# A graph layer with its iterations written out, six groups of places for gathered rows, and the last block of nodes finished early

## The reference

```python
h = jnp.maximum(_layernorm(x, axis=-1), 0.0)
out = h @ W_root + bias
for r in range(8):
    m = (edge_type == r).astype(h.dtype)
    msg = h[src] @ W[r] * m[:, None]
    agg = jax.ops.segment_sum(msg, dst, num_segments=6250)
    cnt = jax.ops.segment_sum(m, dst, num_segments=6250)
    out = out + agg / jnp.maximum(cnt, 1.0)[:, None]
return x + out
```

## Time and profile before

| | |
|---|---|
| time, median of 3 runs | 1579.58 us (1576.46 to 1584.89) |
| the profiled execution, its own time | 1583.01 us |
| its span | 1581.3 us |
| TensorE matmul busy | 753.3 us, 48% |
| weight load busy | 637.7 us, 40% |
| VectorE busy | 729.5 us, 46% |
| ScalarE busy | 511.6 us, 32% |
| GpSimd busy | 758.0 us, 48% |
| mean granted TensorE clock | 0.684 of full |
| row transfers of the late tiles (L464) | 1523 |
| indirect gathers of main tiles | 789 |

### The profile page before, as it was taken

How to read it: one execution, slowest core, us unless ns; L and a number is a source line. 1 busy time by engine, 2 the same in 40 slices (tenths; PEclk the granted TensorE clock), 3 DMA queues, 4 the chain that set the end, 5 groups by cost and what they waited for, 6 DMA issues and landing times.

```text
span 1581.3 us, 24568 instructions
## 1 busy us (share of the span) xinstructions
PE 753.3 (48%) x4265; PEld 637.7 (40%) x4265; DVE 729.5 (46%) x2320; ACT 511.6 (32%) x1183; POOL 758.0 (48%) x809
## 2 busy tenths in 40 slices
PE   0347575574774375466420555645501746742016
PEld 0236454454564254355320444544400545632016
DVE  4747576565564345454420354544510545442007
ACT  3744443433343133343310133433300334331001
POOL 6464566565565365565530255566510566563000
PEclk9967777776676676776755667677655767575556
DMA  6461111111111011111110011111100111111000
GB/s 201 135 151 30 46 43 47 43 48 44 43 44 44 26 44 40 43 45 43 42 29 6 20 44 45 39 43 45 41 19 6 38 44 43 44 44 27 5 7 12
DMA packets 54308, 71.31 MB, mean 45 GB/s; under 512 B 15214, under 2 KB 39550, under 8 KB 54222
## 3 DMA queue, kind: packets, MB, share of 16 engines
q0 software_dynamic: 25248, 51.76, 12.4%
q1 hardware_dynamic: 28974, 18.69, 4.2%
HBM read 63.99 MB, written 6.40 MB: 45 GB/s over the span
## 4 chain that ended last, share of the span: by engine, by line
SPq 54%; issue 36%; DVE 4%; another core or an unknown queue 3%; PE 2%; ACT 1%; DMA 0%; DVEq 0%; POOL 0%; POOLq 0%
SPq L464 46%; SPq L458 6%; PE acc L1620 1%; SPq L450 1%; PE fin L1653 1%; DVE onehot L1106 1%; SPq L443 1%; DVE ring L1120 1%; ACT h_all L625 0%; DMA x_all<-in_x 0%; DVE t_stats L856 0%; DVE stats L835 0%; DVE x_all L1248 0%; PE acc L1624 0%
## 5 line engine op out<-in xcount | busy, mean ns | idle before, releaser
L556 POOL DMA_INDIRECT hg<-h_table,idx x729 | 696.4, 955 | 742.3 <-ACT idx L669 545.7
L1620 PE MATMUL acc<-onehot,hg 128*128 128x104 f32 (+2 forms) x1578 | 454.3, 408 | 104.0 <-issue 43.2
L1620 PEld LDWEIGHTS acc<-onehot,hg 128*128 128x128 f32 x1578 | 325.7, 256 | 153.6 <-issue 74.3
L669 ACT ACTIVATE idx<-src_i 128x3 int32 (+1 forms) x243 | 48.1, 198 | 818.2 <-PE acc L1627 427.6
L1200 DVE SCALAR_TENSOR_TENSOR fin<-ring,zp 128x472 f32<-128x472 f32 x100 | 65.2, 652 | 452.3 <-PE zp L1635 285.7
L1106 DVE TENSOR_SCALAR onehot<-iota,key_f 128x104 f32<-128x104 f32 (+2 forms) x789 | 231.1, 314 | 54.8 <-issue 31.2
L1624 PE MATMUL acc<-onehot,ones_bf 128*128 128x104 bf16 (+2 forms) x789 | 220.6, 280 | 12.0 <-issue 12.0
L1120 DVE TENSOR_TENSOR ring<-ring,acc 128x512 f32 x263 | 178.4, 678 | 96.2 <-remote 40.0
L1642 PE MATMUL zp<-ident,cnt_row 1*118 1x1 f32 x400 | 44.3, 227 | 335.3 <-issue 182.3
L1248 DVE SCALAR_TENSOR_TENSOR x_all<-fin,inv,x_all 118x128 f32 (+1 forms) x400 | 136.8, 342 | 108.0 <-remote 100.4
L1642 PEld LDWEIGHTS zp<-ident,cnt_row 1*118 1x118 f32 x400 | 41.4, 197 | 348.3 <-issue 348.3
(11 more groups left out here) (165 smaller groups left out, 485.9 us busy)
## 6 DMA issues: line engine op xcount, KB each, us to landing
hg<-h_table SPq DMA_DIRECT2D x1523, 0.5 KB
hg<-h_table,idx POOLq DMA_INDIRECT x729
out<-x_all SPq DMA_DIRECT2D x52, 59.0 KB
x_all<-in_x SPq DMA_DIRECT2D x7, 384.0 KB, 3.7
h_table<-h_all SPq DMA_DIRECT2D x7, 384.0 KB
h_all<-h_table SPq DMA_DIRECT2D x5, 504.0 KB
x_all<-in_x SPq DMA_DIRECT2D x5, 504.0 KB
late_src<-in_src SPq DMA_DIRECT2D x47, 0.1 KB
```

Source lines behind the costliest of these rows:

```text
L556: nc.gpsimd.indirect_dma_start(out=hg[:, j, :], out_offset=None, in_=table, in_offset=bass.IndirectOffsetOnAxis(ap=idx[:, j:j + 1], axis=0 ...
L1620: nc.tensor.matmul(both[:, 0, :, a:e], hg[:, slot, :], hot.rearrange("p (r n) -> p r n", r=R), start=(j == 0), stop=(j == n - 1), skip_gro ...
```

## The change

- All iterations are written out: no loops, waits on constants; the `settled` increments are gone from them.
- `hg` holds ten groups first (`FIRST`), then six (`DEEP`) in places 0 to 17; the late tiles use places 18 to 29. POOL waits for `group_summed` itself and reads its indices from `src_i`; `stage` and `idx` are gone. SP begins the late fetch at 10 groups.
- SP fetches two pieces instead of one ahead of every eighth store (`FETCH_MORE`).
- `BLK` is 119, so the last block (number 52) has 62 nodes instead of 114. `LATE_AT` becomes 20, 31, 42, 47. The last block is made from `late_ring` alone in iterations 48 to 50; its neighbours' part of `late_ring` is joined in iteration 51. The block before the last three is finished in `iteration` and no longer in `end`.
- The copies of own rows (`own`) and of counts (`take_counts`) are gone: TensorE reads `h_all` and `ring`.
- ScalarE makes `zeros` and clears the first columns of `ring`; before, POOL and VectorE did.
- The flag that the inputs fit this kernel's plan is made in iteration 16 instead of in the last.

```diff
-BLK = 118
+BLK = 119
-LATE_AT = (20, 31, 42, 51)
+LATE_AT = (20, 31, 42, ENDI - 5)
+LAST_MADE, LAST_LOW, LAST_HIGH, LATE_JOINED = range(ENDI - 4, ENDI)
+FETCH_MORE = 8
+FIRST = 2 * GROUPS
+DEEP = 2 * GROUPS - LATE_GROUPS
...
+        def user_before(g):
+            return g - FIRST if g < FIRST + DEEP else g - DEEP
+        def slot_of(t):
+            return t if t < FIRST * GT else (t - FIRST * GT) % (DEEP * GT)
...
-            for first, last in zip((STATICS,) + tuple(at + 1 for at in LATE_AT[:-1]), LATE_AT):
-                with eng.Fori(first, last) as i:
-                    iteration(i)
-                iteration(last)
+            for i in range(STATICS, ENDI):
+                iteration(i)
             end()
...
-            sp.wait_ge(group_summed, (AHEAD - 1) * GROUPS)
-            for b in range(BLOCKS):
-                if b < chunks_of_late:
-                    fetch_rows(b)
-                store(b, BLK if b < BLOCKS - 1 else LASTN)
+            sp.wait_ge(group_summed, FIRST)
+            fetched = 0
+            for b in range(LASTB):
+                for _ in range(2 if b % FETCH_MORE == FETCH_MORE - 1 else 1):
+                    if fetched < chunks_of_late:
+                        fetch_rows(fetched)
+                        fetched += 1
+                if b == ENDB:
+                    sp.wait_ge(late_step, TERM_STEPS + R + 1)
+                    sp.dma_start(out[LASTB * BLK:N, :], x_all[0:LASTN, LASTB, :]).then_inc(stored, 16)
+                store(b, BLK)
...
+            for t in range(MAIN):
+                g = t // GT
+                if t % GT == 0:
+                    if g == XG:
+                        pool.wait_ge(h_stored, H_STORES)
...
+                    if user_before(g) >= 0:
+                        pool.wait_ge(group_summed, user_before(g) + 1)
+                nc.gpsimd.indirect_dma_start(
+                    out=hg[:, slot_of(t), :], out_offset=None, in_=x if g < XG else table,
+                    in_offset=bass.IndirectOffsetOnAxis(ap=src_i[:, t:t + 1], axis=0)).then_inc(gathered[slot_of(t)], 16)
...
+            nc.scalar.activation(zeros[:, :], eps[:, :].to_broadcast([P, SEG]), ACT.Copy, scale=0.0).then_inc(table_loaded, 1)
+            clear_columns(0)
-            def stage(g, q, ahead):
-                act.wait_ge(group_summed, g + 1)
...
-                nc.scalar.activation(idx[:, q * GT:(q + 1) * GT], src_i[:, bass.ds((g + ahead) * GT, GT)],
-                                     ACT.Copy).then_inc(idx_ready, 1)
...
-            nc.vector.memset(ring[:, :, :, ZERO_CUTS[0]:ZERO_CUTS[1]], 0.0).then_inc(ring_cleared, 1)
...
+                    if static(i, LAST_MADE) and q == 1:
+                        make_late_block(i)
+                    if static(i, LAST_MADE) and q == 3:
+                        late_inverses()
+                    if static(i, LAST_LOW) and q == 3:
+                        add_late_terms(0)
+                    if static(i, LAST_HIGH) and q == 3:
+                        add_late_terms(1)
+                    if static(i, LATE_JOINED) and q == 0:
+                        join_late()
...
+                    if static(i, LAST_MADE) and q == 2:
+                        late_counts()
+                    if static(i, LAST_MADE) and q == 3:
+                        pe.wait_ge(late_step, BLOCK_STEPS + 2)
+                    if static(i, LAST_LOW) and q == 2:
+                        late_relations(0, i)
+                    if static(i, LAST_LOW) and q == 3:
+                        pe.wait_ge(late_step, TERM_STEPS + R // 2)
+                    if static(i, LAST_HIGH) and q == 2:
+                        late_relations(1, i)
+                    if static(i, LAST_HIGH) and q == 3:
+                        pe.wait_ge(late_step, TERM_STEPS + R)
+            def late_relations(half, i):
+                pe.wait_ge(late_step, BLOCK_STEPS)
+                pe.wait_ge(group_added, i * GROUPS - 1)
+                for r in range(half * (R // 2), (half + 1) * (R // 2)):
+                    at = (r % (R // 2)) * F
+                    last = nc.tensor.matmul(last_z[:, at:at + F], last_blk[:, r, :], w_sb[:, r, :], start=True, stop=True)
+                last.then_inc(late_mm, 1)
```

More of the change, by code:

```diff
@@ L549, in gathers @@
[L549 to L557, removed]
-                        in_offset=bass.IndirectOffsetOnAxis(ap=idx[:, j:j + 1], axis=0)).then_inc(gathered[j], 16)
-            pool.wait_ge(src0_i, 1)
@@ L596, in _, with clear_columns @@
             act.wait_ge(table_loaded, 1)
+            nc.scalar.activation(zeros[:, :], eps[:, :].to_broadcast([P, SEG]), ACT.Copy, scale=0.0).then_inc(table_loaded, 1)
+            act.wait_ge(table_loaded, 2)
+            def clear_columns(step):
+                at = slice(ZERO_CUTS[step], ZERO_CUTS[step + 1])
+                for a in range(2):
+                    nc.scalar.activation(ring[:, a, :, at], zeros[:, 0:at.stop - at.start].unsqueeze(1)
+                                         .to_broadcast([P, R, at.stop - at.start]), ACT.Copy).then_inc(ring_cleared, 1)
+            clear_columns(0)
             def deviations(k):
@@ L626, in _ @@
                                          scale=rstd[:, c:c + 1]).then_inc(h_ready, 1)
-            def clear_columns(step):
-                at = slice(ZERO_CUTS[step], ZERO_CUTS[step + 1])
-                for a in range(2):
-                    nc.scalar.activation(ring[:, a, :, at], zeros[:, 0:at.stop - at.start].unsqueeze(1)
-                                         .to_broadcast([P, R, at.stop - at.start]), ACT.Copy).then_inc(ring_cleared, 1)
-            act.wait_ge(fills_made, 1)
             clear_columns(1)
@@ L740, in iteration @@
                 b = block_of(i, LAG)
-                slot = slot_of(b) if b is not None else None
+                slot = ring_slot(b) if b is not None else None
                 for q in range(GROUPS):
@@ L1414, in make_last_block @@
                     dve.wait_ge(blk_made, 2 * b + half)
-                    nc.vector.scalar_tensor_tensor(out=tail_own, in0=ring[:, 1, rs, slot], scalar=LOOP_FLAG / 2, in1=h_b,
+                    nc.vector.scalar_tensor_tensor(out=own, in0=ring[:, 1, rs, slot], scalar=LOOP_FLAG / 2, in1=h_b,
                                                    op0=ALU.is_ge, op1=ALU.mult).then_inc(own_part_made, 1)
-                    dve.wait_ge(z_done, b)
+                    if k != 1:
+                        dve.wait_ge(z_done, b if k == 0 else b - 1)
@@ L1706, in iteration @@
                         tail_products()
+                    if static(i, STATICS - 1) and q == 3:
+                        pe.wait_ge(bad_ready, 1)
+                        pe.wait_ge(group_added, i * GROUPS)
+                        nc.tensor.matmul(badT, bad1[:, :], ones[:, 0:1], start=True, stop=True).then_inc(tail_mm, 1)
                     if part_at(i, q, 3, 1) is not None:
@@ new lines, in last_relations @@
+            def last_relations(k, half):
+                b = TAILB[k]
+                pe.wait_ge(blk_made, 2 * b + 2 if k == 0 else 2 * b + half + 1)
+                if half:
+                    pe.wait_ge(y_ready, b)
+                else:
+                    pe.wait_ge(term_added, terms_before(b - 1) + (R // 2 + 1 if k == 0 else R // 2))
+                for r in range(half * (R // 2), (half + 1) * (R // 2)):
+                    at = (r % (R // 2)) * F
+                    last = nc.tensor.matmul(fin[0:BLK, half, at:at + F], tail_blk[k][:, r, :], w_sb[:, r, :],
+                                            start=True, stop=True)
+                last.then_inc(z_high if half else z_low, 1)
@@ new lines, in late_counts @@
+            def late_counts():
+                pe.wait_ge(late_step, BLOCK_STEPS)
+                for r in range(R):
+                    last = nc.tensor.transpose(last_cntT[:, r:r + 1], late_ring[0:1, 1, r, LAST_AT:LATE_NODES], ident[0:1, 0:1])
+                last.then_inc(late_mm, 1)
+            def late_relations(half, i):
+                pe.wait_ge(late_step, BLOCK_STEPS)
+                pe.wait_ge(group_added, i * GROUPS - 1)
+                for r in range(half * (R // 2), (half + 1) * (R // 2)):
+                    at = (r % (R // 2)) * F
+                    last = nc.tensor.matmul(last_z[:, at:at + F], last_blk[:, r, :], w_sb[:, r, :], start=True, stop=True)
+                last.then_inc(late_mm, 1)
```

345 lines of the change are left out of this document (170 added, 175 removed).

## The result

The changed kernel took 1521.08 us as a median of four executions (1501.4 to 1540.7), the kernel before 1578.02 us on the same chip (1576.36 to 1584.89). The medians' ratio is 0.964; the ratio of 0.955, with an interval of 0.946 to 0.964, leaves out the two executions (1527.3 and 1540.7) that lie over 1.5% above the fastest. The forecast was 1583 us with a range of 1552 to 1622. The profiled execution of the changed kernel is the longest of its four, 1540.7 us with a span of 1538.9, so all that is read from its trace is read from a slow one of them.

A forecast was written before the change was run, and what follows sets the result against it. SP's fetch of the late rows, slowed by gathers, was taken to bound the kernel. Terms -29.8 - 33.6 - 7.4 + 76 - 2 = +3.2 gave a 1584.5 us span, 1583 us on the median's footing; range 1552 to 1622.

The forecast's parts named there:

- The bound: SP's fetch of the last 1523 edges' rows sets the time from 138.5 to 1531.5 us.
- The beginning of the fetch: SP's late fetch waits for 10 groups summed instead of 20 and begins near 108 us: -29.8 us.
- The overlap: Gathers colliding with SP's fetch fall from 711 to 672, with 60 behind it: -33.6 us.
- The price of a gather: SP's delay per colliding gather, 0.861 us before, taken as 0.85 after: -7.4 us; bounds 0.81 and 0.91.
- The footing: The sum starts from the profiled execution, 3.4 us above its median; 1586 us becomes 1583 us on the median's footing.
- The tail: The stretch behind SP's fetch grows from 49.8 to 125.5 us, with 26 groups standing there: +76 us.
- the other engines' traffic makes SP slow: Loops' register instructions and `settled` increments slow SP; removal might halve a gather's price, -286 us, about 1330 us; chance 0.06.
- my two counter-arguments: Against traffic slowing SP: SP stays at 0.70 us while TensorE stands still; the first 17 iterations without loops cost 0.81.
- a cheaper gather: A gather costs SP 0.81 us (-27), or the tail nears 95 us (-30): 1550 to 1565 us; chance 0.25.
- The signs of being wrong: Pieces under gathers below 33 us on average, the 26 groups under 100 us, or SP waiting for stores.
- The speed of the iterations: Faster hand-overs save 1.2 us an iteration, five times behind SP's fetch, -6 us; in the other 47 TensorE only waits longer.
- The rule of the Trainium skill cited in the prediction: Taken branches outside the two-page window cost a fetch; by it all 36 looped iterations gain, -36 us instead of -6.

The follow-up runs named there:

- e18: The changed kernel with the 12 late tiles gathered by GpSimd and SP's 1523 row transfers left out: 1229.12 us, 0.778 of the kernel before.
- e13: The kernel before with its loops written out and without the `settled` increments: 1512.14 us, 0.958 of the kernel before.
- e10: The kernel before with each of SP's 1523 row transfers issued a second time, into a scratch tensor: 1937.59 us.
- e11: The changed kernel with each of SP's row transfers issued a second time, into a scratch tensor: 1990.82 us.
- e17: The changed kernel with three `settled` increments behind each former wait of ScalarE, GpSimd and TensorE: 1604.97 us, 0.9945 of the kernel before.
- e2: The kernel before with its loops written out, the `settled` increments kept: 1026.8 us, 1.0017 of the kernel before.
- e14: The kernel before with its loops written out, the `settled` increments kept, on another chip: 1029.44 us, 1.0022 of the kernel before.
- e16: The kernel before with its loops written out, the `settled` increments kept, on another chip: 1029.08 us, 1.0029 of the kernel before.
- e1: The changed kernel run once more, nothing else changed: 1014.37 us, 0.9905 of the kernel before.
- e9: The changed kernel with three `settled` increments behind each former wait of ScalarE, GpSimd and TensorE: 1016.1 us, 0.9906 of the kernel before.
- e8: The changed kernel run again, nothing else changed, on another chip: 1012.99 us, 0.9884 of the kernel before.

## Why the prediction was wrong, step by step

**The bound: right for the chip that was profiled.** SP's fetch set the time there, and e18 shows it by its absence. On six of the nine chips of the experiments it did not, and nothing in the trace of before tells that.

**The beginning of the fetch: right.** Its first row was due near 108 and came at 107.97; its loads began at 104.3, some 4 us ahead of my reckoning.

**The overlap: right.** 672 forecast, 671 found, 60 behind. The end of the fetch, due near 1460, came at 1410: that is the price again.

**The price of a gather: the step that failed.** "I take 0.85, nearest the whole fetch". It was 0.782: 671 x (0.782 - 0.85) = -46 us, and below my lower bound of 0.81. I had two stretches to choose from: the first at 0.81, "written out", and a later one at 0.91, with regular gathers, and weighed regularity more. The choice rested on a misreading too: GpSimd's own gathers run in a loop from iteration 5 on in the kernel before, not from 17 on, and the increments stand in both stretches, so the stretch at 0.81 was not free of what the change takes away. e13 is, and its first eight pieces show it (GpSimd's gathers, columns as above):

```profile
133.60:391.30 257.70, 162.31 (x169) 0.74 0.17 46
```

(257.7 - 131.2) / 169 = 0.75, where the same pieces and as many gathers cost 0.81 before. So the code of the other engines is part of the price, and 0.81 was no lower bound for a kernel without it. The sum with the measured terms is 104.3 + 781 + 671 x 0.782 + 128.9 = 1538.9, the span (it must be, as the price is what is left of the fetch). My 1584.5 lies 45.6 above it: 46 from the price and some 2 from the beginning (4, of which I had booked 2 under its own head), less 3 in the tail.

**The footing.** The profiled execution before lay 3.4 us above its median; after it lay 19.6 us above it (1540.7 against 1521.08). This makes the rest of the miss, 16 us. The four executions lie 39 us apart, those of before 8.5, and the interval of the ratio is nearly 2% wide. If the fetch is where they differ, which no trace shows, the price in the two fastest (1508 us in the mean) was (1540.7 - 1508) / 671 = 0.05 lower, 0.73 us (an estimate).

**The tail: right, 3 us short.** 26 groups in 113.9 us by the last matmuls of groups, forecast 117 - 6 + 4 = 115, and 9.2 us from the last of them to the end, forecast 10.5. This is the window for TensorE's L1646, and it answers to the earlier trace rows:

```profile
1415.80:1529.70 113.90, 8.17 (x26) 0.73 0.14 39
```

e10 and e11 show the term by itself, +64.5 us where I had +76.

**The rival "the other engines' traffic makes SP slow": right in kind, wrong in size, and given 0.06.** I had it halve the price; it took off 9% here and 11% in e13. Of my two counter-arguments the first was sound and did not bear: SP's pace during a run stays at 0.70 us an instruction in every trace of that kind of chip with the row transfers (before, after, e13, e17), so traffic does not make the slow pace. The second, "the first 17 iterations, with no loops", was the misreading above. I counted what a run costs SP: runs of gathers whose starts lie under 1.6 us apart, with SP's time from one run's start to the next, less 0.5125 us (16.4 / 32) for each row issued in it, in the mean over the fetch:

| | before | e13 | changed | e17 |
|---|---|---|---|---|
| a run of six costs SP, us | 4.42 | 3.79 | 4.53 | 4.65 |
| a run of nine costs SP, us | 8.73 | 7.81 | 8.13 | 8.37 |
| runs of six; of nine; of ten or more | 34; 36; 10 | 43; 44; 2 | 59; 25; 1 | 38; 30; 10 |

In e13 the runs are cheaper. Before and in e13 some 10.5 rows are issued in each cycle of six, whether it takes 9.90 us (before) or 9.11 (e13): the 0.8 us by which the hand-over behind a run is longer bring SP nothing. That the other engines' sequencers are still working off their slow instructions in that time is how I read it; no run shows it directly. In the changed kernel it is otherwise: a run of six costs no less than before (8.7 rows in 8.97 us), but the long runs are nearly gone. With the changed kernel's lengths of runs and the costs of the kernel before, a gather would come to 0.76 us, or 0.80 with its runs of up to three at the changed kernel's own 0.43 us a gather (before has few of them); with e13's lengths, to 0.84. So in the changed kernel most of the gain stands beside shorter runs, and in e13 beside cheaper ones. In e17 the long runs are back, with the increments alone. Both theories of the experiments thus hold a part, and what lengthens a run is open: each kernel has one trace, and relay and depth were not changed alone where a gather slows SP.

**The rival "a cheaper gather", given 0.25,** had the direction, but stopped at 0.81 and 1550 us.

**The signs of being wrong did not show.** Pieces with 14 gathers or more took 35.3 us in the mean, not under 33 (36.1 before, counted from the traces); the 26 groups took 113.9; and SP waited for no store inside the fetch. A piece under gathers was no measure of the price, since in the changed kernel more gathers fell into each (23.4 for 22.7).

**The speed of the iterations: looked for in the wrong place.** I wrote that outside the tail the faster hand-over is worth nothing, since TensorE would only wait longer. It does wait longer, 327.0 us for 280.5; but the hand-over is also part of SP's price, and through it reached the bound.

**The rule of the Trainium skill cited in the prediction** (Runtime: NRT & Kernel Launch, Instruction fetch mechanics) speaks for a gain from written-out iterations; at my 1 us for each of them it was -36 us. The count was wrong as well: 31 iterations are looped on the other engines (17 to 50, without 20, 31 and 42), and 47 on GpSimd. e2, e14 and e16, which change only that, ran at 1.0017 to 1.0029 of the kernel before, where GpSimd is the bound and could hide it. On a chip with the price that kernel was not measured, so what the loops give there stays open, as does a single increment in place of three.

**On the other kind of chip** the change gives 1.0 to 1.2%. First gathers and last gathers of e1 and e2 show where; the tile's timeline in e1, then in e2:

```profile
3.80 1.10 POOL L568 DMA_INDIRECT hg<-in_x,src_i  x1 [0.30 <-DVE src_i L793]
...
995.45 0.94 POOL L568 DMA_INDIRECT hg<-h_table,src_i  x1 [0.30 <-issue]
```

```profile
6.33 1.10 POOL L543 DMA_INDIRECT hg<-in_x,src_i  x1 [1.05 <-DVE src_i L827]
...
998.95 0.94 POOL L554 DMA_INDIRECT hg<-h_table,idx  x1 [0.30 <-issue]
```

GpSimd begins 2.5 us earlier, because VectorE and GpSimd no longer clear `ring` and `zeros` ahead of the first indices, and 1 us more is gained on the way to its last gather. Behind that gather stand 1012.1 - 995.45 = 16.6 us in e1 and 1025.4 - 998.95 = 26.4 us in e2: the last block's own pass is gone from the end. Both parts are read from the traces; neither was tried alone.

## What to carry to other kernels

When one engine's pace depends on what another does, the price of such a collision is no constant: read from the trace what ends the slow stretch, and count the hand-over behind it, and how long the runs are, as part of the price. An instruction that lies off the critical path by its own engine's waits may still be on it that way. And when a term of the sum rests on a behaviour that takes over a third of the time (711 x 0.861 = 612 of 1581 us), run the kernel before on more than one chip first; a version without the collision (12 gathers for 1523 transfers) is worth far more than any tuning around it where the collision exists, and costs 0.4% where it doesn't.

## What the hardware showed that I had not expected

- The kernel before took 1574 to 1624 us on the chips of the profiles on record, of e13, e17 and e18, and 1023 to 1028 us on the six of the other runs, with nothing between. In the first kind an SP instruction takes 0.70 us while GpSimd gathers and a row 0.41 us only in the quiet; in the second a row takes 0.41 us throughout. GpSimd's own gather, 0.95 us and 1.25 us from start to start, is the same in both. What in a chip, or in what else ran on it, makes the difference, no run shows.
- On the first kind, three semaphore increments behind each wait of three engines, some 3500 instructions in all, cost 3 to 4% of the time (e17 against the changed kernel on another chip, each by its ratio to the kernel before); on the second at most 0.2% (e9 against e8, by their ratios).
- A second transfer from the same register brought SP's row from 0.41 to 1.06 us, more than twice: the second issue alone shows as 0.50 us against 0.28 for the first.
